# Gates gathered with the rows, VectorE takes the experts' output, and late groups summed from PSUM in a decoder layer on one core

## What is computed

```python
x = _layernorm(x + attention(x, Wq, bq, Wk, bk, Wv, bv))     # softmax over features (q) and tokens (k, v)
x = _layernorm(x + cross(x, ctx_1024, ctx_1024))             # linear, no softmax
x = _layernorm(x + moe(x, ...))

# moe, per token
probs = softmax(flat @ gate_W.T); top_v, top_i = top_k(probs, 2)      # 8 experts, 2 taken
routed = sum over the two: gate * ((silu(x @ w1_e) * (x @ w3_e)) @ w2_e)
shared = sum over 8 slices: ((silu(x @ w1_s) * (x @ w3_s)) @ w2_s) / 8
return 0.5 * shared + 0.5 * routed
```

## Time and profile before

| | before |
|---|---|
| median of 3 runs | 719.38 us (718.06 to 722.60) |
| profiled execution, its own time | 721.83 us |
| its span, first to last instruction | 720.0 us |
| PE busy | 666.4 us, 93% |
| VectorE busy | 424.2 us, 59% |
| ScalarE busy | 466.0 us, 65% |
| GpSimd busy | 464.2 us, 64% |
| routing stage ends on PE | 282.2 us |
| last expert block's products on PE end, combine begins | 628.2 us |
| PE's last matmul ends | 698.6 us |
| mean granted clock of PE | 0.973 of 2.4 GHz |

### The profile page before, as it was taken

How to read it: one execution, slowest core, us unless ns; L and a number is a source line. 1 busy time by engine, 2 the same in 40 slices (tenths; PEclk the granted TensorE clock), 3 DMA queues, 4 the chain that set the end, 5 groups by cost and what they waited for, 6 DMA issues and landing times.

```text
span 720.0 us, 16573 instructions
## 1 busy us (share of the span) xinstructions
PE 666.4 (93%) x5112; PEld 622.0 (86%) x5113; DVE 424.2 (59%) x1339; ACT 466.0 (65%) x1378; POOL 464.2 (64%) x519
## 2 busy tenths in 40 slices
PE   4899999987999989999999999999999999998970
PEld 2578888886789878999999999999999999987860
DVE  2589999975899888333333333333333333368794
ACT  4899999973347675555556556556556555456795
POOL 2378889896211148777777777777777777524444
PEclk9899999988999999999999999999999999999995
DMA  8457655552312637545545545545554555275563
GB/s 215 132 179 242 198 175 171 167 187 99 125 56 59 172 140 237 179 147 168 163 149 163 166 143 166 168 148 159 168 155 152 168 143 166 68 187 143 151 189 88
DMA packets 98193, 112.55 MB, mean 156 GB/s; under 512 B 11282, under 2 KB 73626, under 8 KB 98138
## 3 DMA queue, kind: packets, MB, share of 16 engines
q1 hardware_dynamic: 88752, 93.28, 42.4%
q0 software_dynamic: 9088, 18.63, 9.3%
q10 hardware_dynamic: 298, 0.01, 0.0%
HBM read 85.80 MB, written 26.08 MB: 155 GB/s over the span
## 4 chain that ended last, share of the span: by engine, by line
PE 71%; DVE 11%; ACT 7%; issue 5%; POOL 3%; DMA 3%; DVEq 0%; SPq 0%; ACTq 0%; POOLq 0%
PE bank L1601 17%; PE bank L1563 9%; PE bank L1564 9%; PE bank L1565 9%; PE bank L555 5%; PE bank L1165 3%; PE bank L550 3%; PE bank L1555 2%; ACT ev L716 2%; PE bank L1154 2%; DVE xg L1913 2%; PE bank L580 2%; PE bank L1155 2%; PE bank L1156 2%; PE bank L575 1%
## 5 line engine op out<-in xcount | busy, mean ns | idle before, releaser
L1695 DVE TENSOR_TENSOR s_hT<-s_sg,bank 128x512 f32<-128x512 f32 x142 | 97.7, 688 | 219.4 <-PE bank L1565 218.7
L1495 POOL DMA_INDIRECT xg<-x_rows,src_tab x142 | 142.6, 1004 | 50.7 <-issue 36.4
L1563 PE MATMUL bank<-e_x_hi,e_w_hi 128*128 128x256 f32 x568 | 172.4, 304 | 0.0
L1503 POOL DMA_INDIRECT y_rows<-e_y,dst_tab x142 | 138.9, 978 | 47.1 <-issue 40.2
L1565 PE MATMUL bank<-e_x_hi,e_w_lo 128*128 128x256 f32 x568 | 160.8, 283 | 0.0
L1564 PE MATMUL bank<-e_x_lo,e_w_hi 128*128 128x256 f32 x568 | 160.7, 283 | 0.0
L1601 PE MATMUL bank<-w,s_hT 128*128 x1136 | 138.3, 275 | 0.0
L1601 PEld LDWEIGHTS bank<-w,s_hT 128*128 128x128 f32 x1136 | 133.1, 192 | 0.0
L1637 ACT ACTIVATE s_sg<-bank 128x512 f32<-128x512 f32 x142 | 84.8, 597 | 38.4 <-PE bank L1565 30.9
L1564 PEld LDWEIGHTS bank<-e_x_lo,e_w_hi 128*128 128x128 f32 x568 | 109.2, 192 | 0.0
L1563 PEld LDWEIGHTS bank<-e_x_hi,e_w_hi 128*128 128x128 f32 x568 | 108.8, 192 | 0.0
(11 more groups left out here) (175 smaller groups left out, 1463.4 us busy)
## 6 DMA issues: line engine op xcount, KB each, us to landing
e_w_lo<-w_lo_rows SPq DMA_DIRECT2D x68, 512.0 KB
yk<-y_rows SPq DMA_DIRECT2D x16, 512.0 KB, 4.5
xT_in<-in_xT_dram SPq DMA_DIRECT2D x16, 256.0 KB, 3.1
x_res<-in_x_dram SPq DMA_DIRECT2D x16, 256.0 KB, 3.3
w_all<-in_L_ffn_w_e_dram SPq DMA_DIRECT2D x16, 256.0 KB, 4.0
c_in<-in_ctx_dram SPq DMA_DIRECT2D x16, 256.0 KB, 2.9
cT_in<-in_ctxT_dram SPq DMA_DIRECT2D x16, 256.0 KB, 3.2
x_rows<-x SPq DMA_DIRECT2D x16, 256.0 KB, 2.4
```

The source lines that it names most:

```text
L1495: nc.gpsimd.indirect_dma_start(xg[b % XR][:, t, :], None, x2_rows, bass.IndirectOffsetOnAxis(src_tab[:, i:i + 1], 0)).then_inc(gathered[b ...
L1503: nc.gpsimd.indirect_dma_start(y_rows, bass.IndirectOffsetOnAxis(dst_tab[:, n:n + 1], 0), y[b % R][:, t, :], None).then_inc(scattered[b % ...
L1563: nc.tensor.matmul(at, w_hi[r % WR][:, w], x_hi[r % R][:, :], start=True, stop=False)
L1695: nc.vector.tensor_tensor(hT[par][:, half * HC:(half + 1) * HC, :].rearrange("p c n -> p (c n)"), sg[half][:, :], bank[2 + half][:, :], AL ...
```

## The change

What it does:

- **Gates travel with the rows.** `x2_rows` becomes 8,192 x 130: behind the 128 features stand the token's two gates. `store_gates` on SP writes them by four DMAs of 128 x 16 x 2 elements, ahead of the load of x2T for group 6; GpSimd waits for them before its first gather. The gather brings rows of 130 elements, and `is_top`, made in `look_back`, says for each slot whether it is the token's first or second choice.
- **The gate is applied in the experts.** VectorE makes `gate` (two operations of 128x1 in `x_low`) and takes y in place of ScalarE, as gate times y plus the row itself. The two results of a token thus sum to 2*x2 plus the routed part doubled; the gates, the shared part and EPS are scaled to match (the layer norm takes out the factor of 2). The gather's ring of 16 is free when y is taken, not when the rows are transposed.
- **Routing.** The loads of `x2_all` go. ScalarE's `keep_shared` copies the shared sums from PSUM to `shared_all`, in place of VectorE's `add_shared`. The Exp moves on ScalarE from behind chunk 27 to behind chunk 8, the `shares` on VectorE from chunks 30, 31 to 12, 13; GpSimd's subtraction for the Exp moves ahead of `x_low` 2 and 3.
- **Combine.** `gate` on ScalarE goes. VectorE's four gated adds become one plain add of 128x512 (`routed`). The late groups' sums are read from PSUM by `total` itself, from banks 4 to 7, so `add_shared` goes; and their turn is spread: the steps 3, 5, ... 15 take the groups 9 to 15, the others the groups 0 to 8 (`ORDER`).

The core of the diff:

```diff
-        x2_rows = nc.dram_tensor("x2_rows", (T, D), F32, kind="Internal").ap()
+        x2_rows = nc.dram_tensor("x2_rows", (T, D + K), F32, kind="Internal").ap()
...
+        def store_gates():
+            sp.wait_ge(gates_ok, K)
+            for q in range(4):
+                at = slice(q * NT // 4, (q + 1) * NT // 4)
+                sp.dma_start(x2_rows.rearrange("(t p) d -> p t d", p=P)[:, at, D:D + K],
+                             gates[:, at, :]).then_inc(gates_stored, 16)
+
         def rest():
             sp.wait_ge(attended.l_ps, NG)
-            for g in range(EARLY):
-                if g + 3 < EARLY:
-                    load_x(g + 3)
-                sp.dma_start(x2_all[:, ds(g * GT, GT), :], group_rows(x2_rows, g)).then_inc(all_ld[g // 2], 16)
-            for g in range(EARLY, NG):
-                sp.dma_start(x2_all[:, ds(g * GT, GT), :], group_rows(x2_rows, g)).then_inc(late_ld, 16)
+            for g in range(3, EARLY):
+                if g == 6:
+                    store_gates()
+                load_x(g)
...
+        def keep_shared(g):
+            act.wait_ge(y_ps, g + 1)
+            nc.scalar.activation(shared_all[:, ds(g * GT, GT), :].rearrange("p t d -> p (t d)"), bank[4 + g % 2][:, :],
+                                 ACT.Copy, scale=2.0 * ALPHA / NS).then_inc(added, 1)
...
-                if n == LOOK + 1:
+                if n == C0 - 2:
                     act.wait_ge(exp_in, 1)
                     nc.scalar.activation(e8[:, :, :], e8[:, :, :], ACT.Exp).then_inc(exp_ok, 1)
+                if n % FC == 1 and n >= 2 * FC:
+                    keep_shared(n // FC - 2)
...
+                c_.link(nc.vector.tensor_scalar(found_i, at_i, shift, 1, ALU.logical_shift_right, ALU.bitwise_and))
+                c_.link(nc.vector.tensor_copy(place, found_i))
+                c_.add(nc.vector.tensor_scalar(is_top[:, :], place, -1.0, 1.0, ALU.mult, ALU.add))
...
             if b >= XR and t == 0:
-                pool.wait_ge(xT_ps, b - XR + 1)
+                pool.wait_ge(y_ok, b - XR + 1)
...
+            for t in range(BT):
+                rows = xg[b % XR]
+                nc.vector.scalar_tensor_tensor(gate[b % (2 * R)][:, t:t + 1], rows[:, t, D:D + 1],
+                                               is_top[:, b * BT + t:b * BT + t + 1], rows[:, t, D + 1:D + 2],
+                                               ALU.mult, ALU.max)
...
+        def take_y(b, j, r):
+            dve.wait_ge(y_ps, b + 1)
+            dve.wait_ge(x_lo_ok, b + 1)
+            if b >= R:
+                dve.wait_ge(scattered[r], 16 * BT * j)
+            for t in range(BT):
+                last = nc.vector.scalar_tensor_tensor(y[r][:, t, :], bank[4 + r % 2][:, t * D:(t + 1) * D],
+                                                      gate[b % (2 * R)][:, t:t + 1], xg[b % XR][:, t, 0:D], ALU.mult, ALU.add)
+            last.then_inc(y_ok, 1)
...
+    late_at = {2 * i + 3: EARLY + i for i in range(LATE)}
+    soon = iter(range(EARLY))
+    ORDER = [late_at[s] if s in late_at else next(soon) for s in range(NG)]
...
+        def routed(g):
+            dve.wait_ge(y_ld[g % R], 16 * (g // R + 1))
+            nc.vector.tensor_tensor(part[g % 2][:, :, :], yk[g % R][:, :, 0, :], yk[g % R][:, :, 1, :],
+                                    ALU.add).then_inc(part_ok, 1)
...
+                i = own - EARLY
+                dve.wait_ge(y_ps, i + 1)
+                nc.vector.scalar_tensor_tensor(z[g % R][:, :, :].rearrange("p t d -> p (t d)"), bank[4 + i % 4][:, :],
+                                               2.0 * ALPHA / NS, part[g % 2][:, :, :].rearrange("p t d -> p (t d)"),
+                                               ALU.mult, ALU.add).then_inc(z_ok, 1)
```

More of the change, by code:

```diff
@@ L1056, in routing @@
     x_ld = [sem(f"r_x_ld{n}") for n in range(2)]
-    all_ld = [sem(f"r_all_ld{n}") for n in range(-(-EARLY // 2))]
-    late_ld = sem("r_late_ld")
+    gates_ok = sem("r_gates_ok")
+    gates_stored = sem("r_gates_stored")
     x_hi_ok = sem("r_x_hi_ok")
@@ L1409, in rest @@
                     place_of(n - PRE - 1)
[L1410 to L1411 removed]
+                if 2 <= n - C0 < 4:
+                    shares(n - C0 - 2)
                 if 0 <= n - LOOK < 2:
@@ L1422, in rest @@
                 ahead(n - EARLY * FC)
-            for g in range(EARLY - 2, EARLY):
-                add_shared(g, g % 2)
             c_.wait()
@@ L1456, in experts @@
     y = ring("y", [P, BT, D])
+    gate = ring("gate", [P, BT], n=2 * R)
     w_lo = ring("w_lo", [P, 2 * F], F32R, n=WR)
@@ L1759, in combine @@
     less = ring("f_less", [P, GT])
-    first, part, res = (m["spare"][n:n + 2] for n in (0, 2, 4))
+    part = pair("part", [P, GT, D])
+    res = pair("res", [P, GT, D])
     st = pair("f_st", [P, GT, 6])
```

114 lines of the change are left out of this document (37 added, 77 removed).

## The result

The changed kernel takes 712.06 us (median of 4 runs, 710.23 to 713.78), the kernel before 720.99 us (median of 4, 718.06 to 723.15, measured beside it): a ratio of 0.9879, 95% interval 0.9844 to 0.9913, or 8.9 us less. The forecast was 9.0 less. The traces put what belongs to the change at 7.1 us.

What follows compares the result with a forecast made beforehand. The prediction took PE to bound the expert blocks, with gains only in routing, combine and its tail. Its terms, +0.8 - 2.0 + 0 - 7.8 = -9.0 us, gave 712.8 for the profiled execution and a forecast median of 710.4, range 706 to 718.

Steps and rivals of the forecast that it cites:

- Routing, start: Start of routing: the moved Exp block delays VectorE, so PE's first table product comes 0.8 us later; bounds 0 and 1.5.
- Routing, end: Late routing: operations removed from VectorE let PE reach the experts 2.0 us earlier; bounds 1.0 and 2.8.
- The wait of 1.75 in chunk 32: Late routing: PE's wait of 1.75 us for s_hT becomes 1.2, and the smaller waits behind it go.
- Gates' stores: Routing: the new 8-byte gate writes, at 33 ns per packet, end by 239 us, hidden; price 0.
- Rival (b): Routing: slow 8-byte writes delay x2T 6, ScalarE and PE; at 66 ns per packet 727 us; chance 0.12.
- Experts: Expert blocks: PE still binds at 4.88 us per block, VectorE's added work is hidden; price 0, bounds 0 and 2.6.
- GpSimd's lag: Experts: GpSimd falls behind PE; 5.1 us (2.0 from the starts, 3.1 from contention) stays below a slack of 5.6.
- rival (a): Experts: small operations cost GpSimd 0.1 us per block, PE stalls 2.6 us late in the stage; 713.0 us; chance 0.15.
- Combine: Combine stage: a shorter ring and shorter VectorE tail groups bring the end 7.8 us earlier; bounds 5 and 10.3.
- ring: Combine: loop from x_high through ScalarE's work, SP's store and loads to x2T's landing holds PE; 11.76 us shrinks to 10.2 and 10.6.
- rival (c): Combine: the ring doesn't shorten, since landing grows from 4.9 to 6 us with closer loads; 712.6 us; chance 0.15.
- Rival (d): Combine and routing: no ring, -10.3 us, and the Exp fits into idle time, -2.0; 707.1 us; chance 0.13.

Runs made afterwards that it cites:

- again: The changed kernel unchanged, measured a second time with a profile of its own: 712.59 us, ratio 0.9908 to the kernel before.
- split_three: The changed kernel with a third buffer for the low halves of routing's weight split, so VectorE waits for an older store: 711.85 us, ratio 0.9876.
- best_low: The changed kernel with late x2T loads issued earlier, GpSimd's softmax subtraction behind x_low 2, and x_low 8 one chunk earlier: 707.55 us, ratio 0.9829.
- gates_more: The changed kernel with the gates stored three times, 12 DMAs instead of 4, the added sets into unread rows: 727.05 us, one run.
- routing_alone: The kernel before with only the Exp, its GpSimd subtraction and VectorE's shares moved: 719.52 us, one run.
- gate_back: The changed kernel with the combine stage's gate put back on ScalarE and four gated adds on VectorE: 716.69 us, ratio 0.9963.
- ring_early: The changed kernel with x2T loads for late groups 4 to 6 issued one step earlier in SP's queue: 710.55 us, ratio 0.9881.
- pool_wide: The changed kernel with a memset of 128x256 added on GpSimd in each expert block: 723.88 us, one run.

## Why the prediction was right, and where it wasn't

The forecast as a whole (8.9 for 9.0 in the first measurement) was better than its parts, and that was luck. Step by step, from the stretches behind the mark:

- **Routing, start (+0.8).** Measured +1.0 to the first table product, but of other things. The Exp's block costs 0.74 alone and 0.14 with add_shared gone (18.97 us from ranks to table in "again", 18.83 before): I had put 1.4 and 0.6. What I had not seen is the 0.84 of the picks: the diff moves GpSimd's subtraction ahead of its x_low, and I read that as a matter of when ScalarE gets its input, not of which VectorE operation lies beside it.
- **Routing, end (-2.0).** The mis-sized term: -0.8 from the first table product on. I counted VectorE's removed operations in a stretch where VectorE is full, as if each came back in full. But GpSimd's x_low, which has its place there in any case, holds VectorE for 1.7 us (1.1 in the kernel before), and PE's fourth table product now comes 0.3 late, behind the sum and reciprocal and behind a one-hot operation that takes 1.69 us in place of 0.74 beside another x_low. The wait of 1.75 in chunk 32 did not become 1.2: PE now waits 0.90 for x_low at the chunk's head and 0.84 for s_hT in its middle, as much in sum. Only the three small waits (0.20, 0.30 and 0.23) went. The other 0.3 of the missing 1.2 I can't place; the alternatives tried (split_three, best_low) moved the stage by 0.2 and nothing. Start and end together: +0.2, not -1.2. The experts did begin 1.1 earlier in "again" (287.34 for 288.44), which looks like the forecast, but the attention ended 1.3 earlier there.
- **Gates' stores (0, at 33 ns per packet).** Price 0 is right, and they landed by 232.3, not 239: at most 23 ns per packet in gates_more. Rival (b), at 66 ns, is out. The Trainium skill (DMA: Bandwidth & Descriptors, Specifications) has such writes done as read-modify-write; at 8 bytes each packet here was no slower than the 33 ns of 530-byte packets in the earlier trace rows, so of a doubled cost these runs show nothing.
- **Experts (0).** The pitch stays (4.87 from 287.34 to 594.23, 63 blocks; 4.88 before), take_y and the gates hide. The stretch is 0.6 shorter, 0.009 us per block, which comes with every kernel that has take_y on VectorE; why, I can't say. GpSimd's lag: I let it grow by 3.1 us, with 2.0 for the two starts, and had 0.5 of 5.6 left. It grew by 1.5 (344.75 us from first to last gather, 343.28 before), the starts came 1.0 closer, and 1.7 were left. So rival (a) did not come and was near, but that it came out near took two errors: both costs were put too high, and so was the slack of 5.6 (by about 1, an estimate: 1.5 + 1.0 + 0.6 for the shorter stretch + 1.7 = 4.8).
- **Combine (-7.8).** Measured -6.7: 4.5 for the gate (ring and tail), 2.4 for order and sum, by the two runs that put them back. Ring 10.38 and 10.20 (10.2 and 10.6 forecast), tail group 2.24 (2.3), chunk 12 without a wait: all as told. The term that was put wrong is x_high of group 4, which I let stay at 658.4 while the routing stage's gain was added to the sum by itself. It stood at 658.33 although the stage began 1.6 earlier, since its load, issued 1.6 earlier too, took 5.92 us to land and not 4.4. That is rival (c)'s mechanism, landing that grows, at the first of the three loads. It is no scatter: with the load at this place, it landed after 5.9 to 6.4 us in all eight profiles without the gate, and after 4.4 to 4.7 in the three with it (before, routing_alone, gate_back). Why is not shown. Rival (d), no ring, was one line of SP's queue away: ring_early took 4.1.
- **The sum.** -9.0 forecast, -7.1 behind the mark. That the first measurement agreed to 0.1 is scatter, for the most part of the attention stage, and so luck; the second gave -6.6. The range (706 to 718) held both.

## What to carry to other kernels

Ahead of a comparison, cut the span at an instruction that the change doesn't touch and compare the stages behind it: here the scatter of an untouched stage, 6 us between profiles, was larger than most of the terms, and medians of six runs could not tell apart what the stretches of two traces did. Look up the granted clock of the stretch as well, and compare more than one profile where a ring passes on every delay. Where an engine waits for a DMA, look at what stands ahead of its issue in the queue before shortening the work that feeds it. When an operation moves on GpSimd, look up what VectorE has at its new place, not only who waits for its result.

## What the hardware showed

- GpSimd's tensor operations and VectorE's on SBUF hold one another up. A subtraction of 1.04 us on GpSimd beside two picks cost VectorE 0.84, one of 1.28 us beside operations of 0.2 to 0.35 us cost it 1.7. It isn't always VectorE that pays: at 216.13 in the kernel before, x_low took 1.88 in place of 1.29 us beside VectorE's one-hots, which ran at their usual length. The Trainium skill names it (GPSIMD Engine Reference, Key points: contention with VectorE instructions in a 2-port mode or with two SBUF inputs); the traces agree, with one source (w_at) and with two (pick, own). Of VectorE's products with a source in PSUM none was stretched (36 s_hT in routing, 0.66 to 0.70 us each).
- A row of 8 bytes cost at most 23 ns per DMA engine, and with many in a row the issue itself was slow: the first four DMAs of 2,048 rows took SP 0.4 to 1.7 us each in gates_more, the eight behind them 2.3 to 3.5.
- PE's idle time in its rows can be less than what it loses: 3.2 us of idle time in the ring of "again" and 4.4 in pool_wide stood for losses of 3.9 and 10.4, and the waits of its weight loads, 3.7 and 9.0, came nearer.
- A short operation on GpSimd between indirect DMAs is nearly free: 0.117 us of memset cost 0.01; one of 0.33 cost 0.2.
- With one and the same attention code, the end of the attention stage came between 183.3 and 189.4 us, with a granted clock of 0.59 to 0.91 from 160 to 180 us.
